# Adding scatter into the residual in HBM, block by block, in place of a two-slot buffer read back and added on VectorE

## The reference, cut to what matters

```
x = x + L0_gnn(layernorm(x), adj, ...)     # graph attention, one head
x = x + L0_ffn(layernorm(x), ...)          # mixture of experts, 8 experts, 2 per token, hidden 256
x = x + L1_gnn(layernorm(x), adj, ...)     # graph attention, 8 heads
x = x + L1_ffn(layernorm(x), ...)          # mixture of experts, 8 experts, 2 per token, hidden 512
```

## Time and profile before

| | us |
|---|---|
| median of 3 runs | 2027.46 |
| lowest, highest | 2022.37, 2035.77 |
| the profiled execution's own time | 2038.51 |
| its span, first to last instruction | 2036.8 |

### The profile page before, as it was taken

How to read it: one execution, slowest core, us unless ns; L and a number is a source line. 1 busy time by engine, 2 the same in 40 slices (tenths; PEclk the granted TensorE clock), 3 DMA queues, 4 the chain that set the end, 5 groups by cost and what they waited for, 6 DMA issues and landing times. The chain is left out here.

```text
span 2036.8 us, 29795 instructions
## 1 busy us (share of the span) xinstructions
PE 1193.0 (59%) x10139; PEld 1024.5 (50%) x10139; DVE 1123.9 (55%) x2503; ACT 995.4 (49%) x1416; POOL 896.0 (44%) x725
## 2 busy tenths in 40 slices
PE   2767676641667762267675666777312206999970
PEld 2656666631556651155554555566212205999860
DVE  2765666552333333579898898999531222343323
ACT  3555555421444431188766866976312204666640
POOL 1011545476355564125325325432467662656550
PEclk8787877765777786578887887888555557999995
DMA  7532332112444443321212111210111125555518
GB/s 240 195 126 84 127 126 86 45 44 94 138 129 128 132 122 104 133 84 73 84 64 74 73 70 68 94 64 32 34 36 46 37 91 155 163 169 163 164 56 247
DMA packets 166117, 213.61 MB, mean 105 GB/s; under 512 B 29812, under 2 KB 121102, under 8 KB 164944
## 3 DMA queue, kind: packets, MB, share of 16 engines
q1 hardware_dynamic: 147792, 175.99, 27.7%
q0 software_dynamic: 18176, 35.72, 5.1%
HBM read 156.71 MB, written 58.56 MB: 106 GB/s over the span
## 5 line engine op out<-in xcount | busy, mean ns | idle before, releaser
L555 POOL DMA_INDIRECT y_dram<-f_ys,f_Xb x312 | 318.0, 1019 | 262.7 <-DVE f_ys L576 180.5
L1469 ACT ACTIVATE g_near<-g_s_row,g_steep 128x1024 fp8e4<-128x1024 f32 x352 | 369.3, 1134 | 2.3 <-issue 2.3
L1444 PE MATMUL g_bp<-g_G,g_near 128*128 128x102 bf16 x4096 | 247.6, 233 | 175.1 <-DVE g_near L1361 175.0
L1444 PEld LDWEIGHTS g_bp<-g_G,g_near 128*128 128x128 fp8e4 x4096 | 239.8, 113 | 203.3 <-issue 201.8
L204 POOL DMA_INDIRECT xs_dram<-r_row,r_pos x256 | 268.4, 1048 | 120.4 <-issue 80.2
L622 PE MATMUL f_ops<-f_w,f_g 128*128 128x128 f32 x1872 | 272.3, 290 | 42.1 <-ACT f_g L658 28.9
L622 PEld LDWEIGHTS f_ops<-f_w,f_g 128*128 128x128 f32 x1872 | 259.0, 204 | 68.8 <-ACT f_g L658 38.4
L658 ACT ACTIVATE f_g<-f_hps,f_ex 128x512 f32<-128x512 f32 x234 | 159.2, 689 | 199.4 <-PE f_hps L614 103.7
L1361 DVE TENSOR_TENSOR g_near<-g_near,g_mask 128x2048 uint32<-128x2048 uint32 x64 | 163.5, 2555 | 50.1 <-ACT g_near L1469 27.5
L1350 DVE TENSOR_SCALAR g_near<-g_s_row,g_nd 128x1024 fp8e4<-128x1024 f32 x160 | 158.3, 1038 | 0.0
L945 PE MATMUL attout<-V,Pt 128*128 128x129 f32 x1024 | 146.9, 304 | 9.5 <-DVE Pt L814 8.5
(11 more groups left out here) (223 smaller groups left out, 2164.1 us busy)
## 6 DMA issues: line engine op xcount, KB each, us to landing
raw<-in_adj SPq DMA_DIRECT2D x64, 512.0 KB, 6.5
g_s_row<-rows_dram SPq DMA_DIRECT2D x64, 512.0 KB, 3.6
f_Xb<-xs_dram SPq DMA_DIRECT2D x78, 288.0 KB
f_w<-in_L_ffn_W SPq DMA_DIRECT2D x78, 256.0 KB
f_yb<-y_dram SPq DMA_DIRECT2D x16, 1024.0 KB, 6.1
f_w<-in_L_ffn_W SPq DMA_DIRECT2D x78, 128.0 KB
mask_dram<-mask SPq DMA_DIRECT2D x16, 512.0 KB, 3.5
g_mask<-mask_dram SPq DMA_DIRECT2D x8, 1024.0 KB
```

What stands on the lines that cost most here:

```text
L555: pool.indirect_dma_start(y_d.rearrange("n k d -> (n k) d"), bass.IndirectOffsetOnAxis(ap=Xb[:, i % XB, r, D:D + 1].bitcast(U32), axis=0), ...
L1444: ins = pe.matmul(bp[h % 2][:, t // 4, (t % 4) * 6 * C:(t % 4 + 1) * 6 * C], near[:, h % 4, j, t * P:(t + 1) * P], G[:, s, j, h, :, :], st ...
L1469: ins = act.activation(near[:, h % 4, j, :], s_row[:, h % 4, :], ACT.Relu, scale=STEEP, bias=steep[:, s, j, h:h + 1], saturate=False)
```

## The change

The ids become plain token numbers, both choices of a token alike. The two-slot tensor `y_d` is gone. Its place is taken by an HBM copy of x for L = 0 (`x1_dram`) and by the output itself for L = 1. The copies of x are stored ahead of the expert layers: for L = 0 batch by batch inside `phase_gat0`, for L = 1 in one DMA of 4 MB at the start of `phase_route`. The scatters at line 555 now add to the destination (`compute_op=ALU.add`). Since two blocks may hold the same token, POOL waits before block i's scatters until those of block i-1 have landed. The loads of `y_d`, the 16 additions on VectorE and the stores of the output at the end of the blocks are removed. `phase_gat1` loads x again from HBM in three pieces (1, 1 and 6 batches).

```diff
@@ router @@
-        pool.iota(idi[:, :, :], pattern=[[1, 2], [2 * P, NT]], base=0, channel_multiplier=2).then_inc(s_c, 1)
+        pool.iota(idi[:, :, :], pattern=[[0, 2], [P, NT]], base=0, channel_multiplier=1).then_inc(s_c, 1)
...
-        dve.tensor_scalar(ids[:, :, :], ids[:, :, :], float(2 * N), None, ALU.add).then_inc(s_t, 1)
+        dve.tensor_scalar(ids[:, :, :], ids[:, :, :], float(N), None, ALU.add).then_inc(s_t, 1)
@@ phase_route @@
             R.sp_setup(sp)
+            sp.dma_start(K["acc"][1], K["x"][:, :, :]).then_inc(s_xst, 16)
             R.sp_params(sp)
             R.sp_pads(sp)
+            sp.wait_ge(s_xst, 16)
@@ phase_blocks @@
-    rows_d, y_d, ex_d = K["xs_dram"], K["y_dram"], K["ex_dram"][L]
+    rows_d, acc_d, ex_d = K["xs_dram"], K["acc_rows"][L], K["ex_dram"][L]
...
-    yb = T("yb", [P, 2, NT, 2, D], FP32)
...
             for i in range(YB):
-                sp.wait_ge(s_ys[i], 64 * (NB // YB))
-            for b in range(B):
-                wait(sp, s_add, 2 * (b - 1))
-                sp.dma_start(yb[:, b % 2, :, :, :], y_d[b * N:(b + 1) * N, :, :].rearrange("(t p) k d -> p t k d", p=P)).then_inc(s_yl[b % 2], 16)
-                if last and b:
-                    sp.wait_ge(s_add, 2 * b)
-                    sp.dma_start(K["out"][:, (b - 1) * NT:b * NT, :], x_sb[:, (b - 1) * NT:b * NT, :]).then_inc(s_out, 16)
-            if last:
-                sp.wait_ge(s_add, 2 * B)
-                sp.dma_start(K["out"][:, (B - 1) * NT:B * NT, :], x_sb[:, (B - 1) * NT:B * NT, :]).then_inc(s_out, 16)
-                sp.wait_ge(s_out, 16 * B)
+                sp.wait_ge(s_ys[i], 64 * len(range(i, NB, YB)))
 
         @block.gpsimd
         def _(pool):
             for i in range(NB):
                 pool.wait_ge(s_ysc, i + 1)
+                if i:
+                    pool.wait_ge(s_ys[(i - 1) % YB], 64 * ((i - 1) // YB + 1))
                 for r in range(4):
-                    pool.indirect_dma_start(y_d.rearrange("n k d -> (n k) d"), bass.IndirectOffsetOnAxis(ap=Xb[:, i % XB, r, D:D + 1].bitcast(U32), axis=0),
-                                            ys[:, i % YB, r, :], None, bounds_check=2 * B * N - 1, oob_is_err=False).then_inc(s_ys[i % YB], 16)
+                    pool.indirect_dma_start(acc_d, bass.IndirectOffsetOnAxis(ap=Xb[:, i % XB, r, D:D + 1].bitcast(U32), axis=0),
+                                            ys[:, i % YB, r, :], None, bounds_check=B * N - 1, oob_is_err=False, compute_op=ALU.add).then_inc(s_ys[i % YB], 16)
...
-            for b in range(B):
-                dve.wait_ge(s_yl[b % 2], 16 * (b // 2 + 1))
-                xb = x_sb[:, b * NT:(b + 1) * NT, :]
-                dve.tensor_tensor(xb, xb, yb[:, b % 2, :, 0, :], ALU.add).then_inc(s_add, 1)
-                dve.wait_ge(s_add, 2 * b + 1)
-                dve.tensor_tensor(xb, xb, yb[:, b % 2, :, 1, :], ALU.add).then_inc(s_add, 1)
@@ phase_gat0, SP @@
+            def store_x(c):
+                sp.wait_ge(s_up, 2 * c + 2)
+                sp.dma_start(K["acc"][0][:, c * NT:(c + 1) * NT, :], x_sb[:, c * NT:(c + 1) * NT, :]).then_inc(s_xst, 16)
+
             def step(b):
                 if b < B - 2:
                     load(b + 2)
                 if b == -1:
                     R.sp_params(sp)
+                if b >= 2:
+                    store_x(b - 2)
                 for hf in range(2):
...
             for b in range(-1, B - 1):
                 step(b)
+            for c in range(B - 3, B):
+                store_x(c)
             for hf in range(2):
                 sp.wait_ge(s_mst[hf], B * 16)
             R.sp_pads(sp)
+            sp.wait_ge(s_xst, B * 16)
@@ phase_gat1 @@
             sp.dma_start(ab[:, :], a.rearrange("(o e) -> o e", o=1).to_broadcast([P, 2 * HD])).then_inc(s_w, 16)
+            for c0, c1, s_in in ((0, 1, s_x0), (1, 2, s_x1), (2, B, s_x2)):
+                sp.dma_start(x_sb[:, c0 * NT:c1 * NT, :], K["acc"][0][:, c0 * NT:c1 * NT, :]).then_inc(s_in, 16)
...
                 if isinstance(b, int) and b == -1:
+                    dve.wait_ge(s_x0, 16)
+                    dve.wait_ge(s_x1, 16)
                     normalise_at(0, STATS)
                     normalise_at(0, NORM)
+                if isinstance(b, int) and b == 0:
+                    dve.wait_ge(s_x2, 16)
@@ build @@
-        K["y_dram"] = nc.dram_tensor("y_dram", (B * N, 2, D), FP32, kind="Internal").ap()
+        x1_dram = nc.dram_tensor("x1_dram", (B * N, D), FP32, kind="Internal").ap()
+        K["acc_rows"] = [x1_dram, out.rearrange("b n d -> (b n) d")]
+        K["acc"] = [v.rearrange("(t p) d -> p t d", p=P) for v in K["acc_rows"]]
```

More of the change, by code:

```diff
@@ L423, in phase_route @@
     R = router(nc, sb, sem, K, L, px, Wr, br, W1, b1, W2, b2, gamma, beta, 3)
+    s_xst = sem("r1_xst")
     with nc.Block() as block:
@@ L488, in phase_blocks @@
     AHEAD, SKEW, GS, XB, WB, YB, TR = 2, 2, 4, 8, 5, 3, 3
-    last = L == 1
-    x_sb, ident, tab = K["x"], K["ident"], K["tab"]
-    rows_d, y_d, ex_d = K["xs_dram"], K["y_dram"], K["ex_dram"][L]
+    ident, tab = K["ident"], K["tab"]
+    rows_d, acc_d, ex_d = K["xs_dram"], K["acc_rows"][L], K["ex_dram"][L]
     S = lambda n: sem(f"f{L}_{n}")
@@ L515, in phase_blocks @@
     s_ys = [S(f"ys{i}") for i in range(YB)]
-    s_yl = [S(f"yl{i}") for i in range(2)]
-    s_add, s_out = S("add"), S("out")
     with nc.Block() as block:
@@ L729, in phase_gat0 @@
     s_neg, s_e, s_up = sem("g0_neg"), sem("g0_e"), sem("g0_up")
-    s_setup, s_wt, s_dv = sem("g0_setup"), sem("g0_wt"), sem("g0_dv")
+    s_setup, s_wt, s_dv, s_xst = sem("g0_setup"), sem("g0_wt"), sem("g0_dv"), sem("g0_xst")
     x_v = x_dram.rearrange("b (t p) d -> p (b t) d", p=P)
@@ L1170, in phase_gat1 @@
     s_prod, s_sum, s_rden, s_on, s_x = (S(n) for n in "prod sum rden on x".split())
+    s_x0, s_x1, s_x2 = (S(n) for n in "x0 x1 x2".split())
     E1, EVAC_E1 = 1, 5
@@ L1527, in build @@
         K["xs_dram"] = nc.dram_tensor("xs_dram", (ROWS, RW), FP32, kind="Internal").ap()
-        K["y_dram"] = nc.dram_tensor("y_dram", (B * N, 2, D), FP32, kind="Internal").ap()
+        x1_dram = nc.dram_tensor("x1_dram", (B * N, D), FP32, kind="Internal").ap()
+        K["acc_rows"] = [x1_dram, out.rearrange("b n d -> (b n) d")]
+        K["acc"] = [v.rearrange("(t p) d -> p t d", p=P) for v in K["acc_rows"]]
         K["ex_dram"] = [nc.dram_tensor(f"ex{L}_dram", (E, P, H // P + 2 + D), FP32, kind="Internal").ap() for L, H in ((0, 256), (1, 512))]
         K["tab"] = keep("tab", [P, 2, NB], I32)
-        K["out"] = out.rearrange("b (t p) d -> p (b t) d", p=P)
         K["rmax"] = bass.bass_isa.ReduceOp.max
```

## The result

The changed kernel takes 2208.21 us (median of 4 runs, 2205.00 to 2210.92) against 2024.91 us (4 runs, 2018.99 to 2035.77): a ratio of 1.090, 95% interval 1.085 to 1.095. It is 183 us slower. The predicted 2066 was far off, and 2200, the upper end of the range, was passed by 8 us.

The account below looks back on a forecast made before the run. TensorE was taken to bound the L = 1 expert stage, nothing that of L = 0; tails were uncovered. Stages 78T + 4 - 527, tails -82, reload +4 gave +39 us at T = 8.2: 2066 us, range 1975 to 2200.

Parts of the forecast that it names:

- T: Period of a block on POOL in the expert stages: three issues, last landing, waking; 6.9 us with plain scatters, 8.2 forecast.
- 78T - 601: Formula for the whole kernel's change in us, from both expert stages, removed tails and reload; zero at T = 7.7.
- the removed tail: Read-back of y_d, additions and output stores after the expert stages: 35 us in L = 0, 47 in L = 1 go.
- x: In the expert stages, what adding puts on top of T: from 0 to 3.9 us, taken as 1.3.
- +0.12 per issue: Each adding scatter's issue on POOL takes 0.12 us longer; +0.5 us per block.
- +0.5 each: Upper bound on POOL's issue: each of four scatters as long as the longest, 1.47 against median 0.97 us; +2.0 together.
- +0.8: Landing of a block's last scatter in us, longer because adding first reads the destination from HBM.
- bound of +1.9: Upper bound on the landing: a whole HBM load's fixed part, 1.9 us, ahead of the write.
- B: Rival: POOL's issue becomes the bound, 0.5 us or more per adding scatter beside slow landing; +171 us, about 2200; chance 0.15.
- A: Rival: adding is nearly free, destination read beside ys, issue stays 0.97 us; -47 us, about 1980; chance 0.32.
- 0.18 us of engine time per issue: POOL's queue share spread over 568 issues and 16 engines; doubling it would put only 0.2 us on the last landing.
- 6.6 and 6.9 us per block: Pace of blocks without the wait in the expert stages: 6.6 us in L = 0, 6.9 in L = 1.

Follow-up runs that it names:

- the later runs: Kernel before and its variants, run later on three other chips; the unedited kernel before takes 1960 us there, not 2025, and the unedited changed kernel 2200.45 us.
- the plain wait: Changed kernel with its wait for the block ahead kept, but scatters that only write instead of adding: 1994.26 us, ratio 1.0176.

## Why the prediction was wrong, point by point

**The frame held.** T, as the stages' 389.0 and 391.9 us with 0.8 more each over 39 blocks, is 10.03; the formula 78T - 601 gives +181 with it, and the profiles differ by 172.4. The 9 us are small errors: the 5 us allowed for POOL at the start of L = 0 did not come, the removed tail gave 75.5 instead of 82, since the closing of a phase is 3.8 us twice where the prediction had 1 and nothing; the reload of x cost 0.6 instead of 4; and 6.5 us less lie ahead of the first scatter, so the stores of x there are hidden, as the 4 MB store is.

**The step that failed is the size of x,** the price of adding on top of T, and in it the term of the issue: 1.3 was taken for x, 3.1 came. Its parts:
- Issue, "+0.12 per issue": measured +0.57 (medians 1.54 and 0.97). The prediction charged it for four issues, +0.5; it was +2.3. The bound above, +0.5 each, was too low as well. It came from the earlier trace rows's longest scatter, read as a rare heavier issue. That scatter was a plain one held up by an operation on VectorE: its 1.47 said nothing about adding. The argument "nearer to the median of 0.97" was thus no evidence either: no row showed an adding issue, and closeness to plain ones was assumed.
- Landing, "+0.8": from the last issue's start it is +1.1 (median 3.3 against 2.2), but 0.57 of this is that issue's own growth, already counted among the four. The landing proper is +0.5. In the quiet last blocks it is nothing: 2.7 - 1.54 is 1.2 us from the issue's end, and so is 2.2 - 0.97. So this term was put too high; its bound of +1.9 held. Why landings in the middle of a stage are longer than the last ones was not tested.
- A third part was left out of the chain of issues, landing and waking. What a landing releases on VectorE runs just when POOL's next issue starts, and holds it up by up to 0.47 us; that is 0.3 a block on average (26.0 us over 78 blocks). It belongs to the wait: with plain scatters the first issue is longer by 0.44 as well.

Together: 2.3 + 0.5 + 0.3 = 3.1. The landing term, too high by 0.3, hid that much of the issue's error.

**The rivals.** B is what happened (issue above 1.4 us, T above 9.3, x = 3, "about 2200"); it had 0.15. Its evidence "some issues last 1.47 already" was wrong for the same reason, so its number came true by luck; and its "slow landing" was the small part. A fell with its issue of 0.97. Its other half, that the read of the destination runs beside that of `ys`, is not refuted: the last blocks' landings from the issue's end are the same with and without adding.

Its premise of 0.18 us of engine time per issue can be tested too, since the traces record every packet. In the two expert stages the packets of POOL's queue take 9.6 us of engine time per issue after the change and 2.5 before, 0.60 and 0.15 us on each of 16 engines: 3.9 times as much. (The 0.18 was the mean with the routing's issues, which are unchanged at 3.5 us.) An adding issue has 144 packets against 32. By the Trainium skill's rule of a second source read (Collectives: The Full Stack, "The bandwidth ceiling: the fold count and why AG ≠ RS ≠ AR") the engine time would have risen to 0.31 at most, as an estimate; it rose by far more, and the larger price is not in the engines at all but in POOL's issue, which that rule does not speak of. The HBM access of the Trainium skill (DMA: Bandwidth & Descriptors, "Latency and other measured facts"), 0.2 us on average and 2 us under high load, holds the landing's +0.5 between its two figures; in the last blocks the trace shows less than either.

**What could have been seen beforehand.** That the issue might be per row was seen ("hardly looks like work per row") and then argued away because the time is constant. But every issue has 128 rows, so a constant time speaks neither for nor against it. And the forecast's gain rested on TensorE and others setting 6.6 and 6.9 us per block; in the later runs the stage of L = 0 runs at 5.3, bound by POOL, so even the plain wait costs 34 us net there (1994 against 1960).

**What was right:** the landing stops nobody before and everybody after; VectorE waits for POOL's scatters, no row of `yb` is left, TensorE is busy less of the L = 1 stage (71%, where "about 80%" went with T = 8.2), and the statistics of graph attention 1 start 8.9 us after its first issue ("some 9").

## What to carry to other kernels

An adding indirect scatter must be priced with its issue on POOL first (here 1.54 us for 128 rows), and then with a landing for each wait that ordering forces; here the saved read-back was worth 74 us and those two cost 314. Disjoint slots with no order among them, and a read-back moved under the next phase with VectorE adding, were faster here. A maximum in a group of durations is no bound of a new operation until it is known what stood beside it.

## What the runs showed of the hardware that was not expected

- An indirect scatter of 128 rows of 512 bytes from SBUF to HBM is issued in 0.97 us when it writes and in 1.54 when it adds. Half rows do not change the 1.54, and neither do padding rows: no issue of the changed kernel takes less than 1.535.
- The packet records show what an issue sends. Adding: 128 packets of one row each (512 bytes, 256 with half rows, 8 for a padding row) and 16 of 4 bytes. Writing: 16 packets, most of them of 4096 bytes, which is eight rows, and 16 of 4 bytes. A 512-byte adding packet takes its engine 0.087 us on average, a 4096-byte one 0.17 to 0.18. No run tells whether the longer issue comes from the packets or from something else in adding.
- From its start a scatter lands in 2.2 us when it writes, in 2.7 to 5.2 with a median of 3.3 when it adds under the wait. From the end of the issue the shortest adding landing, 1.2 us, is no longer than a writing one.
- POOL's issue waits for the end of a two-input SBUF operation of VectorE that is running when it starts, less 0.12 to 0.13 us; one that starts later is not felt. Tensor operations on POOL stretch eight of VectorE's from 2.13 us to 5.54 and 9.61.
- One landing that releases several engines wakes VectorE and SP together, and POOL 0.7 us after them.
